# Setting a planner's table of durations and landings anew, and placing the row-index writes later on GpSimd, in a one-core transformer block kernel

## The reference

```python
x = x + attn_a(layernorm(x))   # 16 heads, q and k 40 wide (8 + 32), full softmax over 512 keys
x = x + ffn(layernorm(x))      # 8 experts 128 -> 512 -> 128 with silu, top-1 gate
x = x + attn_b(layernorm(x))   # 16 heads, two softmaxes of rotated q,k 8 wide, probs = s1 - lam * s2
x = x + ffn(layernorm(x))      # the same expert weights and gate again
```

## Time and profile before

| | |
|---|---|
| median of 3 runs | 1551.88 us (1550.25 to 1568.23) |
| the profiled execution, its own time | 1561.19 us |
| span of its one core | 1559.4 us |
| mean granted TensorE clock | 0.963 of 2.4 GHz |
| PE, DVE, ACT, POOL busy | 1386.8, 1176.1, 1073.4, 702.6 us |
| instructions | 26967 |

### The profile page before, as it was taken

How to read it: one execution, slowest core, us unless ns; L and a number is a source line. 1 busy time by engine, 2 the same in 40 slices (tenths; PEclk the granted TensorE clock), 3 DMA queues, 4 the chain that set the end, 5 groups by cost and what they waited for, 6 DMA issues and landing times.

```text
span 1559.4 us, 26967 instructions
## 1 busy us (share of the span) xinstructions
PE 1386.8 (89%) x9162; PEld 604.2 (39%) x9162; DVE 1176.1 (75%) x2053; ACT 1073.4 (69%) x1938; POOL 702.6 (45%) x768
## 2 busy tenths in 40 slices
PE   7989999899999988999898899999989998998656
PEld 3324333334555332445442323223234535442246
DVE  6757788777777779776778898998997676779333
ACT  3556666666565766787787788887877787887612
POOL 4332433334413654488865443414345775542123
PEclk8999999999999999999999999999999998999969
DMA  2497666855763234645411663112126443310034
GB/s 77 122 264 240 196 220 188 274 157 173 228 173 84 78 107 147 190 138 167 128 31 51 183 204 89 52 39 62 48 70 222 144 125 105 119 42 29 1 114 152
DMA packets 129325, 204.04 MB, mean 131 GB/s; under 512 B 16723, under 2 KB 95280, under 8 KB 129190
## 3 DMA queue, kind: packets, MB, share of 16 engines
q1 hardware_dynamic: 120006, 188.47, 40.4%
q0 software_dynamic: 6016, 12.71, 2.4%
q10 hardware_dynamic: 3168, 1.15, 0.3%
HBM read 123.90 MB, written 76.84 MB: 129 GB/s over the span
## 4 chain that ended last, share of the span: by engine, by line
PE 51%; DVE 13%; POOL 13%; ACT 9%; issue 7%; SPq 3%; DMA 3%; ACTq 1%; another core or an unknown queue 0%; POOLq 0%; DVEq 0%
PE ps L1245 14%; DVE Mb L1561 9%; PE ps L1212 8%; PE ps L1233 8%; ACT P L1435 6%; PE ps L1341 4%; PE ps L1326 4%; POOL ROW L1504 3%; PE ps L1178 3%; PE ps L1253 2%; POOL TH L1842 2%; POOL Z L1844 2%; POOL rs L1784 1%; POOL HL L1801 1%; DVE st L1528 1%
## 5 line engine op out<-in xcount | busy, mean ns | idle before, releaser
L1561 DVE TENSOR_REDUCE Mb<-ps 128x1 f32<-128x512 f32 (+1 forms) x1029 | 923.9, 947 | 202.7 <-PE ps L1212 192.0
L1435 ACT ACTIVATE P<-ps 128x512 f32<-128x512 f32 (+1 forms) x1237 | 795.1, 710 | 211.8 <-PE ps L1233 176.8
L1212 PE MATMUL ps<-STK 32*128 32x512 f16 (+1 forms) x1536 | 383.6, 387 | 45.1 <-DVE Mb L1561 16.4
L1233 PE MATMUL ps<-STK 32*128 32x512 f16 (+1 forms) x1536 | 391.7, 386 | 29.3 <-ACT P L1435 17.8
L1245 PE MATMUL ps<-P,V 128*32 128x512 f32 x3072 | 407.7, 613 | 3.1 <-ACT P L1435 2.8
L1212 PEld LDWEIGHTS ps<-STK 32*128 32x128 f16 (+1 forms) x1536 | 104.0, 93 | 322.2 <-DVE Mb L1561 116.3
L1233 PEld LDWEIGHTS ps<-STK 32*128 32x128 f16 (+1 forms) x1536 | 105.7, 93 | 210.3 <-ACT P L1435 76.4
L1245 PEld LDWEIGHTS ps<-P,V 128*32 128x32 f32 x3072 | 64.8, 108 | 128.5 <-issue 112.8
L1835 POOL DMA_INDIRECT xs<-ROW,slot x64 | 63.9, 998 | 95.1 <-DVE slot L1652 78.8
L1799 POOL CAST HL<-RT 128x512 f16<-128x512 f32 x47 | 28.7, 611 | 169.0 <-ACT RT L1381 149.1
L1326 PE MATMUL ps<-XT,WE 128*128 128x128 f32 x696 | 95.0, 282 | 5.9 <-ACT XT L1465 2.7
(11 more groups left out here) (160 smaller groups left out, 1396.6 us busy)
## 6 DMA issues: line engine op xcount, KB each, us to landing
WE<-wx SPq DMA_DIRECT2D x87, 576.0 KB
STK<-qka SPq DMA_DIRECT2D x56, 480.0 KB
qka<-HL SPq DMA_DIRECT2D x84, 256.0 KB, 4.8
STK<-qkb SPq DMA_DIRECT2D x64, 256.0 KB
xs<-pad SPq DMA_DIRECT2D x8, 1554.0 KB, 8.2
qkb<-HL SPq DMA_DIRECT2D x96, 128.0 KB, 2.4
X<-xs SPq DMA_DIRECT2D x73, 129.5 KB
qka<-HL SPq DMA_DIRECT2D x42, 128.0 KB
```

The costliest lines, as they stand in the source:

```text
L1212: mm = eng.matmul(ps[:, bank + i, :], l_, r_, start=True, stop=True)
L1233: mm = eng.matmul(ps[:, bank + i, :], l_, r_, start=True, stop=True)
L1435: eng.activation(P[:, st % 3, j:j + n, :], ps[:, bank:bank + n, :], ACT.Exp, scale=SCALE_A if g < 4 * B else SCALE_B).then_inc(sem("exp"), 1)
L1561: eng.tensor_reduce(Mb[:, g % 2, at:at + 4 * n - 3:4], ps[:, bank:bank + n, :], AX, ALU.max).then_inc(sem("mx"), 1)
```

## The change

Three things change. The table gets other durations for 21 stages, from gpsimd's `ln_apply` (2.4 to 3.14) and `ln_rstd` (0.6 to 1.36) to `xcopy` (0.16 to 0.26), and `normal` gets others where it is placed. The landings get others: `put` 3.0 to 5.5 in part A and 2.6 in part B, `stack` 3.0 to 7.0 in part A and 3.2 in part B, `rows` 3.8 to 4.2. And `index(b)` for b of 4 and more is no longer asked for right behind `xload(b)`, but once `gturn(b)` is placed, in a chain of its own. The core of the diff:

```diff
-    "rowmax": ("vector", 1.13), "normal": ("vector", 0.6), "join": ("gpsimd", 0.8), "split": ("gpsimd", 1.6), "ln_stats": ("vector", 1.3),
-    "ln_apply": ("gpsimd", 2.4), "ln_apply_q": ("vector", 1.45), "columns": ("vector", 3.0),
-    "resid": ("vector", 0.68),
-    "gate_max": ("vector", 0.5), "gate_pick": ("vector", 0.2), "gate_slot": ("vector", 0.3), "route": ("vector", 0.35),
-    "xcopy": ("scalar", 0.16), "plus_b2": ("vector", 0.35), "silu_b": ("vector", 0.68), "combine": ("vector", 0.28),
+    "rowmax": ("vector", 1.13), "normal": ("vector", 0.74), "join": ("gpsimd", 0.73), "split": ("gpsimd", 1.85), "ln_stats": ("vector", 1.3),
+    "ln_apply": ("gpsimd", 3.14), "ln_apply_q": ("vector", 1.45), "columns": ("vector", 3.0),
+    "resid": ("vector", 0.605),
+    "gate_max": ("vector", 0.5), "gate_pick": ("vector", 0.3), "gate_slot": ("vector", 0.42), "route": ("vector", 0.47),
+    "xcopy": ("scalar", 0.26), "plus_b2": ("vector", 0.35), "silu_b": ("vector", 0.605), "combine": ("vector", 0.27),
...
-    "index": ("gpsimd", 0.4), "ln_rstd": ("gpsimd", 0.6), "turned": ("gpsimd", 8.4), "silu_p": ("gpsimd", 2.8), "b_lo": ("gpsimd", 2.7), "scatter": ("gpsimd", 4.1), "send": ("gpsimd", 1.1),
+    "index": ("gpsimd", 0.2), "ln_rstd": ("gpsimd", 1.36), "turned": ("gpsimd", 7.4), "silu_p": ("gpsimd", 2.64), "b_lo": ("gpsimd", 2.27), "scatter": ("gpsimd", 4.9), "send": ("gpsimd", 1.0),
...
+def lands(stage, index, hop):
+
+    if stage == "stack" and index[0] < 4 * B:
+        return 7.0
+    if stage == "put" and index[0] >= NA * B:
+        return 2.6
+    return LANDS.get(stage, hop)
...
-            yield from do(rank, "index", b)
+            if b < 4:
+                yield from do(rank, "index", b)
+            else:
+                spawn(numbered(b))
+
+    def numbered(b):
+        yield from after(("gturn", (b,)))
+        yield from do(first_of(b + 1), "index", b)
...
-        end = start + us + LANDS.get(stage, hop)
+        end = start + us + lands(stage, index, hop)
```

More of the change, by code:

```diff
@@ L198 @@
+    "xcopy": ("scalar", 0.26), "plus_b2": ("vector", 0.35), "silu_b": ("vector", 0.605), "combine": ("vector", 0.27),
     "lambda_sums": ("vector", 0.5), "lambdas": ("vector", 0.3), "bias_parts": ("vector", 0.5),
-    "expo": ("scalar", 0.49), "mcopy": ("scalar", 0.18), "ocopy": ("scalar", 0.49), "hcopy": ("scalar", 0.49), "raw": ("scalar", 0.5), "fhi": ("scalar", 0.5),
-    "vcopy": ("scalar", 0.5), "b_hi": ("scalar", 1.0), "acopy": ("scalar", 0.49), "gcopy": ("scalar", 0.49),
-    "gate_exp": ("scalar", 0.25), "silu_z": ("scalar", 0.48), "weigh": ("scalar", 0.2), "plus_p": ("gpsimd", 0.5), "mix": ("vector", 1.4), "wsum": ("tensor", 0.86), "silu_t": ("scalar", 0.49), "lambda_exp": ("scalar", 0.25),
@@ L202 @@
-    "index": ("gpsimd", 0.4), "ln_rstd": ("gpsimd", 0.6), "turned": ("gpsimd", 8.4), "silu_p": ("gpsimd", 2.8), "b_lo": ("gpsimd", 2.7), "scatter": ("gpsimd", 4.1), "send": ("gpsimd", 1.1),
+    "expo": ("scalar", 0.49), "mcopy": ("scalar", 0.18), "ocopy": ("scalar", 0.49), "hcopy": ("scalar", 0.49), "raw": ("scalar", 0.5), "fhi": ("scalar", 0.585),
+    "vcopy": ("scalar", 0.58), "b_hi": ("scalar", 1.05), "acopy": ("scalar", 0.49), "gcopy": ("scalar", 0.49),
+    "gate_exp": ("scalar", 0.25), "silu_z": ("scalar", 0.48), "weigh": ("scalar", 0.265), "plus_p": ("gpsimd", 0.46), "mix": ("vector", 1.4), "wsum": ("tensor", 0.86), "silu_t": ("scalar", 0.49), "lambda_exp": ("scalar", 0.25),
@@ L208 @@
 HOP = {"tensor": 0.21, "vector": 0.13, "scalar": 0.14, "gpsimd": 0.15, "sync": 0.05}
-LANDS = {"direct": 2.5, "xload": 4.0, "setup": 3.0, "put": 3.0, "stack": 3.0, "mput": 2.0, "weights": 5.0, "rows": 3.8, "blank": 6.0, "weights_b": 4.0,
+LANDS = {"direct": 2.5, "xload": 4.0, "setup": 3.0, "put": 5.5, "stack": 3.2, "mput": 2.0, "weights": 5.0, "rows": 4.2, "blank": 6.0, "weights_b": 4.0,
          "weights_p": 3.0, "wload": 14.0, "wstore": 8.0, "scatter": 4.0, "fill": 5.0, "send": 4.0}
@@ L410, in norms @@
                     yield from after(("join", (added(g) - 2,)))
-            yield from do(g + late, "normal", g, us=0.6 if g >= 4 * B else 0.8)
+            yield from do(g + late, "normal", g, us=0.72 if g >= 4 * B else 0.84)
             give("oturn", g)
```

## The result

The change made the kernel slower. Over 20 runs each, the changed kernel took 1569.78 us in the median (1560.28 to 1580.9) and the kernel before 1554.74 us; the ratio is 1.0089 with a 95% interval of 1.0065 to 1.0113, so 0.9% or about 14 us. The forecast was 12 us faster. The profiled execution of the changed kernel took 1564.99 us with a span of 1563.2, 3.8 us more than before.

The account below looks back on a forecast made before the run. PE was taken as the bound in part A, shared with DVE and ACT in part B. 10.4 + 4.9 + 2.4 - 3.7 - 1.2 = 12.8 us, rounded to 12, gave 1540 us from 1551.88; range 1524 to 1563.

Parts of the forecast that it names:

- The norm pair: PE's turns waiting for POOL's ln_apply: longer ln_rstd and ln_apply win two thirds of 15.6 us of waits, 10.4 us.
- The stacks: PE's waits for stacks in part A, 8.3 us in 2 places: the 7.0 us landing wins 4.9 us.
- xcopy: PE's up-projection waits 3.6 us in 6 places for xcopy: 0.26 in place of 0.16 wins 2.4 us.
- The index write: POOL's 17.2 us of waits for the earlier scatter vanish, but waits for DVE and ACT replace them: sum 0.
- The figures that shrink: Slack lost on silu_p, turned and b_lo: -3.7 us from doubled waits and -1.2 us for turned; bound -24.6.
- Rival 2: silu_p and turned come late wherever they had padding, gains come only in part: 1568 us; chance 0.10 (1558 to 1575).
- The shuffle: Reordering of the greedy planner's lists: none charged beyond rounding 12.8 down to 12; plus or minus 6 in rival 1.
- rival 1: PE's gaps filled but waits reappear for DVE's maxima or ACT's exponential: 1552 us; chance 0.27 together with rival 5.
- Rival 3: Later put and stack landings delay part A's first smax of batches 1 to 7 by 6.5 us: 1585; chance 0.05.
- Rival 5: Turn waits stay, coming from stages before ln_apply: 4.9 us or less won, 1547 to 1552; chance 0.27 with rival 1.

Follow-up runs that it names:

- the four drawings with the old durations: Kernel before with only the index write moved, only the landings, TURN at 0.0971, or TURN at 0.096: 1.0050, 1.0155, 1.0103, 1.0021.
- norm_shrink: Kernel before with ln_rstd 1.36, ln_apply 3.14 and GpSimd's shortened figures (silu_p, turned, b_lo, send, plus_p, join): 1.0053.
- e5_dur_silu_28: Kernel before with all the new durations except silu_p, which stays at 2.8: 1.0074.
- after_send_18: Changed kernel with send at 1.8 instead of 1.0, nothing else changed: 0.9849 against the kernel before, 1531.1 us in the median.

## Why the prediction was wrong

*The norm pair, 10.4 us.* Right in mechanism. The 15.6 us of waits fell to 1.0 in the changed kernel and to 0.6 with the pair alone. The size is right only against the list of before, and there by some luck: the pair alone came to 0.7% or 10.4 us, over three drawings 0.8%. Against the four drawings with the old durations, 0.8% slower than before in the mean, the pair is worth 1.6% or some 25 us, more than the bound of 15.6. A gain that was put too low and a loss from redrawing that was put at nothing left about the forecast figure between them.

*The stacks, 4.9 us.* Right for the waits. The wait at the start fell from 6.89 to 4.03 us, with a score of the earlier group ahead of it as forecast, and the second wait is gone; in sum 8.3 to 4.0 us. A gain in time from it is not seen on top of the pair.

*xcopy, 2.4 us.* Too high: 3.6 to 2.5 us of waits. It decides nothing.

*The index write, 0.* Right by the comparison with equal compute lists (1.0098 and 1.0089, whose intervals overlap). That it came out at 1.0050 by itself is put down to the list drawn anew. The sign that the prediction named for it came only in part: L1777's wait is gone, but POOL's waits for DVE's mv and ACT's RT did not grow by 17.2 us; they fell from 319.9 to 307.6.

*The figures that shrink, -4.9 us.* This is the first step that failed: the term was sized too small, because the price of a block on GpSimd was read wrongly. The prediction charged a doubling of the wait for silu_p's result (3.7 more) and 1.2 for turned. The wait grew by 7.0 to 10.7 us. The kernels with the shortened figures and the pair are 1.1 to 1.2% or some 18 us slower than those with the pair and without them; about 11 of these lie in the stretches of the second and third segment (161.4 against 154.0 us and 276.4 against 273.0 in the means), and where the rest lies is open. So the term was two to four times the 4.9 us, within the prediction's bound of 24.6. The prediction compared each new figure with the busy time of its own stage, 2.64 with 2.56 and 7.4 with 7.66, and found them fair. It never compared the block's 4.85 us with the sum of its stages. Setting send to 1.8 was worth 37 us (1.0089 to 0.9849) on the changed kernel and 30 (1.0053 to 0.9857) on norm_shrink. This is not the price of the shortening, since it also mends what the old table lacked. A redrawn list is in both steps, so their size is known to some 20 us, their sign and their place by the wait and the stretches. Rival 2 named these figures, had 0.10 and put the time at 1568 us, where 1569.78 was measured; the reason behind its sum, padding lost on silu_p and turned, was not the whole, as e5_dur_silu_28 showed, so the near hit is partly luck.

*The shuffle, charged at nothing.* This is the second step that failed. The prediction said that it would be wrong if the shuffle were worth more than the named waits; it gave this no chance of its own and, in rival 1, a size of plus or minus 6 us. In two redrawings of the old table it is worth 0.2 and 1.0%, both to the slow side, and 0.8% or 12 us in the mean of the four drawings from the old durations. The list of before is better than any of these four, so a change to its table starts behind. Why that list is the best of its kind was not tried. The 12 us is as large as the whole forecast gain. The changed kernel's own list is also one of the slower drawings of its table: redrawn, it took 1.0017.

*Rival 3, stacks held back.* Not seen: the changed kernel was 10.9 us ahead at group 30, and on the pair no cost of the landings is seen. The landings alone were 1.55% slower, outside the other redrawings; whether the old table has a special fault with them stays open.

*Rival 1 and 5.* Rival 5 fell with the waits of the turns. Rival 1's sign came: PE's idle time is 1563.2 - 1386.3 = 176.9 us, more than the 172.6 of before, although the waits for ln_apply, the stacks and xcopy fell by 14.6 + 4.3 + 1.1 = 20 us. The wait for Z grew by 7.0, but what grew most is PE's waits for ACT's exponentials (P), from 37.8 to 56.5 us over the lines that have them, with over half of the growth here (before had 17.8 us in 47 places):

```profile
PE ps L1250 <- ACT P L1452: 28.4, 63, 2.3
```

Those for DVE's Mb grew from 25.7 to 29.5. Rival 1's reason for them, gaps that are filled and won nothing, does not hold: with the pair alone the same waits are 40.2 and 24.8 us, and the gain is kept. after_send_18 has 42.4 for P, and norm_shrink 41.6, so they came neither with the pair nor with the shortened figures by themselves. Which part of the changed table or of its drawing made them grow stays open.

## What to carry to other kernels

Set a planner's table of durations from the time that a stage holds its engine, from start to start along a chain on one engine, and not from busy times: a pause before an instruction that waits for its own engine's last result belongs to it. Here two kernels with the pause put in were 2.0 and 2.4% faster than those without. Check the sum over a repeated unit, here one expert block, before any single figure. And where a greedy planner writes the order, draw the unchanged kernel several times with a figure altered that has no bearing, and judge a change by the mean of drawings and by the wait that it aims at: here one drawing against the list of before said little below 1.4%.

## What the runs showed of the hardware

An indirect DMA issued by GpSimd right behind the instruction that makes its data starts 0.77 to 0.79 us after that instruction ends in the timelines of the changed kernel and norm_shrink; the waits of before have 18.3 + 16.3 = 34.6 us in 44 places, 0.79 us each. Between the two halves of silu_p, where the second needs the first's result and is an ordinary instruction, the gap is 645.72 - 645.64 = 0.08 us.

TensorE's granted clock fell to the lower of its two levels, 1.2 GHz, for some 17 us in the midst of a busy stretch, from about 608 to 625 us. Windows of the changed kernel, columns as in the earlier trace rows:

```profile
600.00:605.00 5.00, 4.29 (x34) 1.14 (x33) 4.36 (x6) 3.78 (x9) 0.71 (x1) 1.00 0.82 238
605.00:610.00 5.00, 3.94 (x19) 0.89 (x21) 3.81 (x5) 2.00 (x5) 0.00 (x0) 0.81 0.61 216
610.00:615.00 5.00, 4.63 (x20) 1.61 (x20) 3.16 (x4) 3.12 (x7) 0.00 (x0) 0.50 0.53 177
615.00:620.00 5.00, 3.72 (x19) 0.44 (x11) 4.53 (x5) 2.05 (x4) 0.00 (x0) 0.50 0.71 228
620.00:625.00 5.00, 4.32 (x21) 2.39 (x22) 1.89 (x4) 2.64 (x6) 0.00 (x0) 0.50 0.88 297
```

Ahead of the fall PE waited for ACT for 0.69 us at 604.9 and for 0.47 us at 606.2. The kernel before has such falls too, with 0.91 and 0.83 in the windows from 600 to 620 and 620 to 640 us. The time of an execution goes with the clock: the 20 of the changed kernel run from 1560.28 us at a mean clock of 0.962 to 1580.9 at 0.949, and a line through them has 1.24 us per 0.001. Their mean clock is 0.956, while the kernel before has 0.960 to 0.963 in the five sets of executions taken beside the experiments. By these numbers an estimated 5 to 9 us of the 15 between the medians go along with a lower clock. Whether an idle gap brings the clock down and so costs more than its length, or the lists that came out slow did so by this, no experiment shows.
